# Block stage of a fused attention and feed-forward kernel: x turned by transposing DMAs, projections over five PSUM banks, K projection of the next tile moved ahead of the value weighing

## What is computed

```python
h = _L0_tok_ref(x)
h = h + _L0_attn_ref(_layernorm(h), Wq, Wk, Wv, Wo, qn_w, kn_w)
h = h + _L0_ffn_ref(_layernorm(h), w1, w2, w3)
```

## Time and profile before

| | |
|---|---|
| median of 3 runs | 1176.52 us |
| the profiled execution | 1181.81 us |
| its span | 1179.9 us |
| TensorE busy | 1097.3 us, 93% |
| VectorE busy | 722.2 us, 61% |
| ScalarE busy | 422.4 us, 36% |
| GpSimd busy | 433.5 us, 37% |

### The profile page before, as it was taken

The page is one execution under the profiler, slowest core; times in us unless marked ns, Lnnn a source line. Parts: engine busy times, 40 slices in busy tenths (PEclk is TensorE's granted clock), DMA queues, the critical chain, the costliest instruction groups (busy, mean ns, idle before and its releaser), DMA issues.

```text
span 1179.9 us, 22172 instructions
## 1 busy us (share of the span) xinstructions
PE 1097.3 (93%) x8768; PEld 609.3 (52%) x8768; DVE 722.2 (61%) x1293; ACT 422.4 (36%) x733; POOL 433.5 (37%) x334
## 2 busy tenths in 40 slices
PE   4999998889989569999999999999999999999987
PEld 2434333343334234664665756646646657566465
DVE  6687766766686255556655755665566557656642
ACT  1666545545555221322322412323223223223231
POOL 2001016664555254242351451433423614524320
PEclk9999898989998779999999999999999999999999
DMA  6988833554442100000000000000000000000000
GB/s 181 315 298 260 299 115 115 158 176 124 140 130 69 57 9 10 20 9 27 18 9 27 0 27 18 9 27 18 9 27 18 9 27 0 27 18 9 18 11 9
DMA packets 35767, 83.81 MB, mean 71 GB/s; under 512 B 4496, under 2 KB 5264, under 8 KB 35728
## 3 DMA queue, kind: packets, MB, share of 16 engines
q1 hardware_dynamic: 35728, 83.26, 22.8%
HBM read 49.43 MB, written 8.39 MB: 49 GB/s over the span
## 4 chain that ended last, share of the span: by engine, by line
PE 51%; DVE 8%; issue 4%; POOL 2%; ACT 0%; DMA 0%; SPq 0%; DVEq 0%; POOLq 0%
PE proj L973 7%; PE proj L974 7%; PE proj L975 7%; PE ffn_sum L1025 5%; PE ffn_sum L1026 5%; PE proj L1087 4%; PE proj L1088 4%; PE proj L1089 4%; PE transposed L967 3%; PE ffn_sum L1073 2%; PE transposed L1041 1%; PE proj L1059 1%; PE proj L1060 1%; DVE probs_t L930 1%; DVE scores L910 1%
## 5 line engine op out<-in xcount | busy, mean ns | idle before, releaser
L334 DVE TENSOR_REDUCE row_max<-score_rows 128x1 f32<-128x512 f32 x256 | 167.7, 686 | 94.0 <-PE score_rows L474 92.6
L700 POOL TENSOR_TENSOR roped<-rope_cos,rope_sin 128x512 f32<-128x512 f32 x80 | 101.7, 1271 | 328.3 <-DVE rope_sin L836 328.3
L293 ACT ACTIVATE exps<-score_cols 128x512 f32<-128x512 f32 x256 | 146.2, 600 | 140.4 <-PE score_cols L499 137.9
L1025 PE MATMUL ffn_sum<-x_hi,ffn_w 128*128 128x128 f16 x1408 | 167.0, 220 | 1.4 <-ACT x_hi L769 1.4
L1026 PE MATMUL ffn_sum<-x_lo,ffn_w 128*128 128x128 f16 x1408 | 166.8, 220 | 0.0
L735 ACT ACTIVATE squares<-proj 128x512 f32<-128x512 f32 x80 | 47.8, 597 | 323.4 <-PE proj L975 289.5
L973 PE MATMUL proj<-attn_slots,x_hi 128*128 128x512 f16 x384 | 147.8, 385 | 3.7 <-DVE rope_sin L836 2.2
L974 PE MATMUL proj<-attn_slots,x_hi 128*128 128x512 f16 x384 | 147.7, 385 | 0.0
L975 PE MATMUL proj<-attn_slots,x_lo 128*128 128x512 f16 x384 | 147.5, 384 | 0.0
L474 PE MATMUL score_rows<-k_parts,q_parts 96*128 96x512 f32 x256 | 127.4, 511 | 16.5 <-DMA k_parts<-qk_low 15.2
L1025 PEld LDWEIGHTS ffn_sum<-x_hi,ffn_w 128*128 128x128 f16 x1408 | 138.1, 98 | 6.4 <-DVE hidden L853 3.0
(11 more groups left out here) (108 smaller groups left out, 1724.7 us busy)
## 6 DMA issues: line engine op xcount, KB each, us to landing
raw_ffn<-in_w_ffn SPq DMA_DIRECT2D x24, 704.0 KB, 7.2
attn_slots<-in_w_attn SPq DMA_DIRECT2D x20, 512.0 KB, 10.8
qk_raw<-in_qk SPq DMA_DIRECT2D x16, 512.0 KB, 5.8
q_parts<-qk_high SPq DMA_DIRECT2D x32, 256.0 KB, 3.3
k_parts<-qk_high SPq DMA_DIRECT2D x32, 256.0 KB, 4.2
v_t<-in_v_t SPq DMA_DIRECT2D x16, 256.0 KB, 5.7
q_parts<-qk_low SPq DMA_DIRECT2D x16, 256.0 KB, 4.9
k_parts<-qk_low SPq DMA_DIRECT2D x16, 256.0 KB, 5.2
```

The lines of the kernel that those rows point to most:

```text
L293: nc.scalar.activation(E[:, (STEPS * g + u) % NE, :], ST[(STEPS * g + u) % 3][:, :], ACT.Exp, scale=TOK_SCALE).then_inc(exp_done, 1)
L334: nc.vector.reduce_max(row_max[:, g % 2, k:k + 1], S[n % NS][:, :], AX.X).then_inc(s_free, 1)
L1025: nc.tensor.matmul(dst, w, x2h[:, k * P:(k + 1) * P], start=(k == 0), stop=False)
```

## The change

Parts, in the order of the tile:

1. The rows are no longer turned on TensorE. ScalarE casts xn (or x2n), still by rows, to the high part; the low part of x comes from GpSimd (`x_low`, from VectorE before), that of x2 from VectorE. SyncE then issues a transposing DMA for each of the two parts (SBUF to SBUF, 128x512 fp16). TensorE waits for both to land.
2. The six projections go to five banks: K and P3 to PROJ[0], P4 to PROJ[1], P1 and P2 to FB[2] and FB[3], V to TR[1].
3. ScalarE's cast of x2n moves from after `square(n, 3)` to before `square(n, 2)`; VectorE's low part of x2 moves ahead of `rotate(n, 3)`.
4. VectorE's `ln_apply` for tile n+1 moves from after the scores' maxima to after the first `hidden_lo`; ScalarE's cast follows the last copy of q.
5. K of tile n+1 moves from between D10 and O to before W, and `DOWN_FIRST` goes from 8 to 4: D0 to D3, K, W, D4 to D10, O.

```diff
-        BANK_OF = (0, 0, 1, 0, 1, 0)
-        DOWN_FIRST = 8
+        BANK = (PROJ[0], FB[2], FB[3], PROJ[0], PROJ[1], TR[1])
+        DOWN_FIRST = 4
...
+            def turn_x2(n):
+                sp.wait_ge(x2_hi, n + 1)
+                sp.dma_start(x2h[:, :, :], x2hr[:, :], transpose=True).then_inc(x2_turned, DMA)
+                sp.wait_ge(x2_lo, n + 1)
+                sp.dma_start(x2l[:, :, :], x2lr[:, :], transpose=True).then_inc(x2_turned, DMA)
...
                 if ffn:
+                    turn_x2(n - 1)
+                if more:
+                    turn_x(n + 1)
+                if ffn:
                     sp.wait_ge(o_out, n + START)
                     sp.dma_start(out[bass.ds((n - 1) * P, P), :], o_tile[:, :]).then_inc(out_done, DMA)
...
                 if not (isinstance(n, int) and n + 1 >= NTT):
                     inv_std(n + 1, 0, ln1_var, ln1_rstd)
+                    x_low(n + 1)
                     rope_sum(n + 1, 0)
...
             def take_x(n):
-                act.wait_ge(xt, n + 1)
-                nc.scalar.copy(xh[:, :], TR[0][:, :]).then_inc(x_hi, 1)
+                act.wait_ge(ln1, n + 1)
+                nc.scalar.copy(xhr[:, :], xn[:, :]).then_inc(x_hi, 1)
...
             def project(n, c):
 
                 if c == 0:
-                    pe.wait_ge(x_hi, n + 1)
-                    pe.wait_ge(x_lo, n + 1)
+                    pe.wait_ge(x_turned, 2 * DMA * (n + 1))
...
+                if c in (1, 2) and not first:
+                    pe.wait_ge(c_lo, BT * n)
...
             def gate_products(n, f, m):
 
                 if f == 0 and m == 0:
-                    pe.wait_ge(x2_hi, n + 1)
-                    pe.wait_ge(x2_lo, n + 1)
+                    pe.wait_ge(x2_turned, 2 * DMA * (n + 1))
...
                 if ffn:
                     down_products(n - 1, range(0, DOWN_FIRST))
                 if attn and not last:
-                    transpose_x(n + 1)
+                    project(n + 1, 0)
                 if attn:
                     weigh_values(n, ffn)
                 if ffn:
                     down_products(n - 1, range(DOWN_FIRST, KF))
                 if attn:
-                    if not last:
-                        project(n + 1, 0)
                     output_products(n, ffn)
```

More of the change, by code:

```diff
@@ L595, in blocks @@
         xn = sb("xn", [P, D])
-        xh, xl = sb("x_hi", [P, D], F16), sb("x_lo", [P, D], F16)
+        xhr, xlr = sb("x_hi_rows", [P, D], F16), sb("x_lo_rows", [P, D], F16)
+        xh, xl = sb("x_hi", [P, KD, P], F16), sb("x_lo", [P, KD, P], F16)
         sq = [sb(f"squares{n}", [P, D]) for n in range(2)]
@@ L616, in blocks @@
         x2n = sb("x2n", [P, D])
-        x2h, x2l = sb("x2_hi", [P, D], F16), sb("x2_lo", [P, D], F16)
+        x2hr, x2lr = sb("x2_hi_rows", [P, D], F16), sb("x2_lo_rows", [P, D], F16)
+        x2h, x2l = sb("x2_hi", [P, KD, P], F16), sb("x2_lo", [P, KD, P], F16)
         th = sb("tanh", [P, D])
@@ L676, in _, with turn_x @@
                 sp.dma_start(dst, src).then_inc(const_in, DMA)
+            def turn_x(n):
+                sp.wait_ge(x_hi, n + 1)
+                sp.dma_start(xh[:, :, :], xhr[:, :], transpose=True).then_inc(x_turned, DMA)
+                sp.wait_ge(x_lo, n + 1)
+                sp.dma_start(xl[:, :, :], xlr[:, :], transpose=True).then_inc(x_turned, DMA)
+            def turn_x2(n):
[3 more added lines that the diff above has]
+                sp.dma_start(x2l[:, :, :], x2lr[:, :], transpose=True).then_inc(x2_turned, DMA)
+            turn_x(0)
             def body(n, attn, ffn):
-                if attn and not (isinstance(n, int) and n + 1 >= NTT):
+                more = attn and not (isinstance(n, int) and n + 1 >= NTT)
+                if more:
                     sp.wait_ge(ln1, n + 1)
@@ L685, in body @@
                 if ffn:
+                    turn_x2(n - 1)
+                if more:
+                    turn_x(n + 1)
+                if ffn:
                     sp.wait_ge(o_out, n + START)
                     sp.dma_start(out[bass.ds((n - 1) * P, P), :], o_tile[:, :]).then_inc(out_done, DMA)
-            over_tiles(sp, body)
+            for n in range(NTT + 1):
+                body(n, n < NTT, n > 0)
             sp.wait_ge(out_done, DMA * NTT + START)
@@ L707, in rope_sum, with x_low @@
                 nc.gpsimd.tensor_tensor(view, view, bcast(rr[:, of], [P, G, HD], 2), ALU.mult).then_inc(q_ready, 1)
+            def x_low(n):
+                pool.wait_ge(x_hi, n + 1)
+                nc.gpsimd.tensor_tensor(xlr[:, :], xn[:, :], xhr[:, :], ALU.subtract).then_inc(x_lo, 1)
             pool.wait_ge(const_set, 1)
             inv_std(0, 0, ln1_var, ln1_rstd)
+            x_low(0)
             rope_sum(0, 0)
@@ L764, in body @@
                 if attn:
-                    for c in range(1, KV):
-                        square(n, c)
[L767 to L771, removed]
+                    square(n, 1)
+                if ffn:
+                    act.wait_ge(ln2, n)
+                    nc.scalar.copy(x2hr[:, :], x2n[:, :]).then_inc(x2_hi, 1)
+                if attn:
+                    for c in range(2, KV + 1):
+                        square(n, c)
                     act.wait_ge(proj, NPROJ * (n + 1))
-                    nc.scalar.mul(v[:, :], PROJ[BANK_OF[NPROJ - 1]][:, :], V_SHIFT).then_inc(v_out, 1)
+                    nc.scalar.mul(v[:, :], BANK[NPROJ - 1][:, :], V_SHIFT).then_inc(v_out, 1)
                 for f in range(NF):
@@ L783, in body @@
                             nc.scalar.activation(pr[:, :, :], sd[:, :, :], ACT.Exp).then_inc(exped, 1)
+                        if attn and not last and (f, m) == (1, 0):
+                            take_x(n + 1)
                         if ffn and m == 1:
@@ L885, in body @@
                 if attn:
-                    for c in range(2, KV):
-                        rotate(n, c)
+                    rotate(n, 2)
                 if ffn:
                     dve.wait_ge(x2_hi, n)
-                    nc.vector.tensor_tensor(x2l[:, :], TR[1][:, :], x2h[:, :], ALU.subtract).then_inc(x2_lo, 1)
+                    nc.vector.tensor_tensor(x2lr[:, :], x2n[:, :], x2hr[:, :], ALU.subtract).then_inc(x2_lo, 1)
                 if attn:
-                    rotate(n, KV)
+                    for c in range(3, KV + 1):
+                        rotate(n, c)
                     if not last:
@@ L898, in body @@
                     hidden_lo(n - 1, 0)
+                if attn and not last:
+                    ln_apply(n + 1, 0, h_ln[:, :], xn[:, :], ln1_rstd, ln1)
+                if ffn:
                     gate(n - 1, 1)
@@ L918, in body @@
                                             ALU.subtract).then_inc(sub, 1)
-                    if not last:
-                        ln_apply(n + 1, 0, h_ln[:, :], xn[:, :], ln1_rstd, ln1)
                 if ffn:
@@ L934, in body @@
                 if attn:
-                    if not last:
-                        x_low(n + 1)
                     for b in range(2):
@@ L980, in project @@
                 if c == 0:
-                    pe.wait_ge(x_hi, n + 1)
-                    pe.wait_ge(x_lo, n + 1)
-                if c == 0 and not (isinstance(n, int) and n == 0):
-                    pe.wait_ge(v_out, n)
-                if c == 1:
+                    pe.wait_ge(x_turned, 2 * DMA * (n + 1))
+                first = isinstance(n, int) and n == 0
+                if c == 0 and not first:
+                    pe.wait_ge(squared, 5 * n - 1)
+                    pe.wait_ge(roped_b, 5 * n - 1)
+                if c == 3:
                     pe.wait_ge(squared, 5 * n + 1)
                     pe.wait_ge(roped_b, 5 * n + 1)
-                if c == 2 and not (isinstance(n, int) and n == 0):
+                if c in (1, 2) and not first:
+                    pe.wait_ge(c_lo, BT * n)
+                if c == 4 and not first:
                     pe.wait_ge(h2_done, n)
-                if c >= 3:
-                    pe.wait_ge(squared, 5 * n + c - 1)
-                    pe.wait_ge(roped_b, 5 * n + c - 1)
+                if c == NPROJ - 1 and not first:
+                    pe.wait_ge(taken, n)
                 pairs = []
@@ L996, in project @@
                           else Q_AT + k * HEADS * HD + (c - 1) * D)
[L997 to L1009, removed]
+                    pairs.append((xh[:, k, :], xl[:, k, :], W.hi(at, D), W.lo(at, D)))
+                split_products(BANK[c][:, :], pairs, proj)
             def gate_products(n, f, m):
                 if f == 0 and m == 0:
-                    pe.wait_ge(x2_hi, n + 1)
-                    pe.wait_ge(x2_lo, n + 1)
+                    pe.wait_ge(x2_turned, 2 * DMA * (n + 1))
                     pe.wait_ge(c_hi, KV * (n + 1))
@@ L1024, in gate_products @@
                         dst = FB[2 * (f % 2) + m][:, j * P:(j + 1) * P]
-                        nc.tensor.matmul(dst, w, x2h[:, k * P:(k + 1) * P], start=(k == 0), stop=False)
```

(8 more changed lines are left out.)

14 lines of the change are left out of this document (4 added, 10 removed).

## The result

| | before | after |
|---|---|---|
| median | 1176.04 us (4 runs) | 1213.01 us (4 runs, 1212.52 to 1218.59) |
| ratio | | 1.0325 (95% interval 1.0299 to 1.0351) |
| profiled execution | 1181.81 us, span 1179.9 | span 1210.9 |
| block stage, from VectorE's first instruction in it to the end | 783.9 us (396.03 to 1179.9) | 817.4 us (393.49 to 1210.9) |

The change makes the kernel 37.0 us slower; the forecast was 41.4 us slower, 1218 us, in a range of 1196 to 1248. Between the two traces the block stage grew by 33.5 us, while the token stage, which the change doesn't touch, ended 2.5 us earlier.

What follows compares the result with a forecast made beforehand. TensorE was taken to bound the block stage; 14 middle tiles at +2.53 us (35.4), tile 15 +2.7, end +2.75, start +2.7, first tile -2.2 gave +41.4 on 1176.5: 1218 us, range 1196 to 1248.

Steps and rivals of the forecast that it cites:

- What K had covered: Between D10 and O: without K there, O starts at W + 6.47 instead of W + 5.08, 1.39 us lost a tile.
- Removed transposes and K ahead of W: TensorE: transposes gone, 0.88 us a tile; G 12.95 us after P1 starts; W moves to G + 17.47, 0.17 won.
- The way to x2 and to x: x2's low part ends at t0 (P1's start) + 11.22, leaving 1.55 us cover before G; x's cover before K 4.5.
- The price of a transposing DMA: Ahead of G: a transposing DMA takes 3.3 us to land, so TensorE waits 1.75 us a tile.
- Waits that cost more than their length: Rival, chance 0.10: gaps lower TensorE's clock; one fall per tile, 15 x 1.7, adds 25 us: 1243 us.
- a granted clock under 1.00 in the middle tiles: Sign looked for in TensorE's profile after the change; seeing it would prove the prediction wrong.
- Start and end: Outside the middle tiles: the end loses 2.75 us, the first K about 2.7, the first tile wins 2.2.
- P1's gap of 2.17 us: First tile: P1 no longer waits for a rotate, so 2.2 us are won, once.

Runs made afterwards that it cites:

- K back: The change with K of the next tile back between D10 and O and DOWN_FIRST 8: 1182.9 us, ratio 1.0046 to the kernel before.
- x2 early: The change with x2's low part made ahead of rotate 2 instead of behind it: 1199.4 us, ratio 1.0178 to the kernel before.
- ctx_lo first: The change with all four ctx_lo ahead of the output tile in VectorE's list: 1186.4 us, ratio 1.0083 to the kernel before.
- K back and x2 early: The change with K between D10 and O, DOWN_FIRST 8, and x2's low part ahead of rotate 2: 1169.8 us, ratio 0.9927 to before.
- three edits: The change with x2's low part ahead of rotate 2, all ctx_lo ahead of the output tile, O written to FB[0]: 1162.5 us, ratio 0.9880 to before.

## Why the prediction was right, and where its terms were off

The sign, the size and the cause held. By the steps of the text:

- **What K had covered**: right to the hundredth, since the last tile of before had shown the same chain. O came at W + 6.47, the idle time is 2.17 us, released by ctx_lo. Two runs confirm it from both sides: K back takes 1.44 us a tile away, and the reordered ctx_lo 1.10.
- **Removed transposes and K ahead of W**: right for G, which with x2 early follows P5 without a wait. W came at G + 17.56 instead of G + 17.47, 0.09 us a tile. The probabilities end at G + 17.3 and were not ready by G + 17.1: VectorE's 0.53 us less ahead of them mostly turned into waiting for TensorE's scores and for the exponential, which don't move.
- **The way to x2 and to x**: right. The low part of x2 ended at t0 + 11.27 for 11.22 forecast, GpSimd's low part of x at G + 10.2 for 10.3, and K never waits for its turn in a middle tile.
- **The price of a transposing DMA**: mis-sized, the failed term. 3.3 us taken, 2.4 measured. The wait at G is 0.81 us (13.76 - 12.95) and not 1.75. The nearest row was not the copy inside SBUF of 256 KB but the store of this stage at 2.0. The copy's row comes from the token stage, where the DMA engines are busy, against a share of 0.05 in the earlier trace rows; that this is why it lands later isn't shown. With the measured wait in the sum a tile is 48.05; measured 48.15. At 14 tiles the term was 13 us too large.
- **Waits that cost more than their length**: the rival came true in part. Three middle tiles lost 1.7 us each and tile 15 lost it twice. It isn't every tile, so 5.1 us in the middle and 3.4 in tile 15 instead of 25. The sum had no falls in it, and the text itself named a granted clock under 1.00 in the middle tiles as a sign of being wrong: in this point it was. It also overlooked that in tile 15, with no K between D3 and W, TensorE stands idle 2.33 us ahead of W; the first of that tile's two falls came right behind this gap.
- **Start and end**: the end lost 2.9 (2.75 forecast), in part by luck. The way from x2n to G lost 2.3, since the turn lands sooner than taken, and another 0.6 went into gate products at the lower clock. The start to the first h gained 2.8 us where a loss of 0.5 was forecast. The first K came 1.9 us later after xn, not 2.7, and its twelve matmuls took 1.0 us less because more of them ran at the full clock. P1's gap of 2.17 us went as forecast, and with it the clock fall behind it: the two stretches from 410 to 420 us, 0.76 and 0.90 in the earlier trace rows, are at 1.00 after.

```profile
410.00:415.00 5.00, 5.00 (x25) 2.24 (x23) 4.88 (x10) 1.19 (x2) 4.69 (x5) 1.00 0.00 0
415.00:420.00 5.00, 5.00 (x25) 2.23 (x23) 4.17 (x11) 1.19 (x2) 4.71 (x5) 1.00 0.00 0
```

The ledger between the traces: 14 x 1.68 = 23.5, falls 5.1, tile 15 4.8 (3.4 of it falls), end 2.9, start -2.8: +33.5, as the stage's lengths say. The 1218 was closer to the 1213 than its terms were: the DMA's 13 us too much stood against 8.5 us of falls that the sum left out. That is luck and no merit of the sum.

Open stays the rest of 3.5 us to the difference of the medians. The profiled execution of before lay 5.8 us over its median, and the time at which the block stage begins varies between traces of kernels with the same token stage (396.0 before, 393.5 after, 387.1 with ctx_lo first). That spread is larger than the rest, and no run was made on it.

## What to carry to other kernels

When work is moved earlier on the bounding engine, ask first what it covered where it stood: here 2.6 us of K stood between a sum's end and the three operations that had to follow it, and its move cost more (1.44 us a tile) than the transposes saved (0.88 at most). Before such a move, take out of the follower's list all that doesn't depend on the new last product (two ctx_lo), and give the next accumulation a bank of its own. A transfer put in place of an engine's step has to be started one landing (2.4 us here) ahead of its use, and the step that feeds it must not queue behind work that can wait.

## What the runs showed of the hardware

- A transposing DMA of 128x512 fp16 inside SBUF lands 2.4 us after its issue and holds SyncE's queue for 1.2 to 1.3 us, against 0.34 us for a plain store. Two of them one behind the other (issued 1.25 us apart, at 767.79 and 769.04) took 2.4 and 2.5 us.
- Behind a gap of 2.17 us in each tile TensorE's clock went down in 3 of 14 tiles (twice: with the change and with x2 early), behind one of 2.9 us in 6 of 14, behind gaps of 1.1 and 0.7 us never, at 1.6 to 1.7 us each time. All twelve of these falls came between 0.1 us before and 1.4 us after the end of a gap. Each count is one execution's; another execution of the change took 1218.6 us. With the change the falls came every fifth tile (near 492, 734 and 977 us), though the gaps are alike. In tile 15 the same gap of 2.57 us ahead of O stands in three kernels: a fall followed with K back and with K back and x2 early, none before. So the length of a gap isn't all that decides; what else does, the runs don't say.
- Where the long gaps of the middle tiles went, the falls went too (K back, ctx_lo first, three edits). The move of two ctx_lo was worth 1.1 us a tile by the shorter gap, and 5.1 us more in the middle tiles by the clock.
